# A gated state-space layer on one core: bounds widened two tiles ahead, and the carried state kept on 128 rows

## The chip, the cores and the metric

The kernel runs on one core of one Trainium2 chip. The metric is the device time of one execution in microseconds (us). PE is the matrix engine (PEld its weight loads), DVE the vector engine, ACT the scalar engine, POOL the general-purpose engine, and SP the engine whose queue issues the DMAs. Each engine runs its own instructions in order and waits on semaphores for the others.

## What is computed

Two sequences of 2048 tokens (512 features) go through a gated layer with 1024 inner features and a state of 16 x 1024 per sequence:

```python
xr, gate = jnp.split(x @ W_in.T, 2, axis=-1)
xr = xr + t_emb[:, None, :]
xc = silu(causal_depthwise_conv4(xr) + b_conv)
xn = layernorm(xc) * ln_g + ln_b
Bm, Cm, dt = jnp.split(xn @ W_xproj.T, 3, axis=-1)      # 16 each
Ad = 1.0 + 0.01 * tanh(dt @ W_dt.T + b_dt) * -tanh(A_log)
Bd = Bm * minimum(norm(xn), 1.0)
def step(h, inputs):                                     # h is 16 x 1024
    ad, bd, xt, ct = inputs
    h = clip(h * ad[:, :, None] + bd[:, :, None] * xt[:, None, :], -10.0, 10.0)
    return h, einsum('bd,bdh->bh', ct, h)
y = scan(step) + D * xn
out = x + (y * silu(gate)) @ W_out.T
```

## The kernel before

The tokens are cut into 32 chunks of 128 (the two sequences take turns). A chunk has 1024 x 16 scans, cut into 32 tiles: tile number u*4+q holds feature block u (128 features on the partitions) and states 4q to 4q+3, each over 128 tokens, so a tile is 128 x 512. One loop body per chunk `k` has 32 **steps** `s`, and every engine walks through them in its own order. A step has two **points**, 2s and 2s+1.

The way of one tile:

- PE `fill` (L538, four matmuls): the lower bounds of the scan into one of five PSUM banks, `ps_fill`. At step s it fills tile s+3 (`AHEAD`); it first waits for `scanned` of the tile five before (`RING`).
- ACT `copy_low` (L778): copies that bank to `low`. This is the first thing ACT does in a step, for tile s+3. After it come the side jobs of the step's two points.
- PE `widen` (L547, one matmul): adds the width of the bounds to the bank, so that it holds the upper bounds. It waits for `low_copied` of its tile. It is the first thing PE does in a step, ahead of `fill`. Before, step s widens tile s+1.
- DVE `scan` (L984): a max/min scan over `low` and the bank. DVE scans tile s+1 at step s.
- POOL `weigh` (L1082): times C, into one of `HOLD` = 4 buffers `prod`; a buffer is free when its tile is flipped.
- PE `flip` (L574, four transposing matmuls that sum into `ps_y`): tile s-4 at step s. Two tiles (0 and 16) are flipped one step later, together with the next.

Between these stand PE's other matmuls, by the table `JOBS` of (first point, number of parts, name, half, chunk offset, ...): PE does the part of an even point ahead of the step's flip, and that of an odd point behind it. They prepare the next two chunks: `xr` and `gate` (L450, L455, input projection), `conv` (L468, transposes of the taps), `xt`, `z`, `zT`, `nb` (L475), `carry` (L478), and close the last one: `hend` (L482, the state at a chunk's end), `yT`, `out` (L492). They share two banks, `ps_job`; a job waits till the job before it in its bank is taken. `TAKE` gives the point at which ACT or DVE takes a result, and `TAP_AT` the eight points at which ACT makes the four taps of a conv block (L737, into one of `TAPRING` = 3 buffers).

The state between chunks is `h1`, 16 rows x 1024. `hend` turns the chunk's last columns (`kend`) with 8 transposes, and DVE subtracts `lend` in two halves (L891). The job `h0` has a bank and no matmul: ACT writes `x0` times the first B into the bank (L704; `x0` is token 0 of the normalized input, sent by a DMA to 16 rows), DVE adds `h1` times the first decay (L918) and clips to `h1` (L931), again in two halves at points 16 to 22. The second half's L704 waits till the first half's L931 is done. ACT and POOL then split `h1` into two half-precision parts (L722, L1055).

Of the kernel before, what the change touches and what calls it, by code (L numbers as in the profile page):

```python
# [42 lines left out]
HOLD = 4  # L43
TAPRING = 3
# [25 lines left out]
xT_in xT_high xT_low tap_done conv_part x0_in0 x0_in1 spans_clear w_piece0 w_piece1 w_piece2 w_piece3 w_high w_low  # L70
# [10 lines left out]
y_gated h0_sum carry16  # L81
h0_ready h0_taken h1_in0 h1_in1 decay0 h1_high h1_low
# [3 lines left out]
def build(nc, A, out, scratch, r_dram, c_dram):  # L86
    F, H = mybir.dt.float32, mybir.dt.float16
    ALU, ACT = mybir.AluOpType, mybir.ActivationFunctionType
    with ExitStack() as S:
# [17 lines left out]
        small = sb("small_sb", [NS, 3 * NS + 2])  # L107
# [33 lines left out]
        first_decay = sb("first_decay", [NS, 1])  # L141
# [12 lines left out]
        h1 = sb("h1", [NS, DI])  # L154
        lend = sb("lend", [NS, 2, DI])
# [4 lines left out]
        h16 = sb("h16", [NS, 2, DI], H)  # L160
        x0 = h16[:].rearrange("n h d -> n (h d)").bitcast(F)
# [11 lines left out]
        kend = sb("kend", [P, 2, DB, NS])  # L173
# [24 lines left out]
        JOBS = [(3, 2, "z", 0, 1, 1, 1), (3, 4, "gate", 0, 0, 2, 0), (6, 1, "hend", 0, -1, 2, 1),  # L198
                (8, 4, "gate", 1, 0, 2, 0), (8, 1, "hend", 1, -1, 2, 1), (10, 1, "yT", 1, -1, 2, 1),
                (15, 1, "zT", 0, 1, 1, 1), (19, 4, "xr", 0, 2, 2, 0), (16, 1, "h0", 0, 1, 2, 1),  # L200
                (25, 4, "xr", 1, 2, 2, 0), (21, 1, "h0", 1, 1, 2, 1), (25, 1, "nb", 0, 1, 1, 1),
                (33, 11, "conv", 0, 2, 2, 0), (30, 1, "carry", 0, 1, 2, 1), (35, 1, "carry", 1, 1, 2, 1),
                (40, 13, "out", 0, -1, 1, 1), (46, 9, "conv", 1, 2, 2, 0), (54, 1, "yT", 0, 0, 2, 1),
                (57, 1, "xt", 0, 2, 2, 0), (60, 1, "xt", 1, 2, 2, 0)]
        LAST = {(name, i): first + parts - 1 for first, parts, name, i, *_ in JOBS}
        TAKE = {("z", 0): 5, ("gate", 0): 7, ("hend", 0): 6, ("hend", 1): 8, ("yT", 1): 10, ("gate", 1): 12,
                ("zT", 0): 15, ("h0", 0): 16, ("h0", 1): 20, ("xr", 0): 23, ("nb", 0): 25,
                ("xr", 1): 29, ("carry", 0): 30, ("carry", 1): 35, ("conv", 0): 44, ("out", 0): 53,
                ("conv", 1): 55, ("yT", 0): 54, ("xt", 0): 58, ("xt", 1): 62}
        TAP_AT = [26, 31, 33, 36, 39, 42, 45, 49]  # L210
# [52 lines left out]
        def first_chunk(j):  # L263
            return isinstance(j, int) and j < BATCH
# [10 lines left out]
        def _(sp):  # L275
            for dst, src in ((c128[:], A["c128"]), (cols[:], A["cols"]),
                             (wx, A["wxT"].rearrange("(c p) m -> p c m", p=P)), (small[:], A["small"]),
                             (h1[:], A["wx_dt"])):
                sp.dma_start(dst, src).then_inc(sem["const_in"], 16)
# [26 lines left out]
            def body(k, p):  # L306
# [21 lines left out]
                if exists(k, 1):  # L328
                    j, pn = k + 1, (p + 1) % 2
                    xstack, stack = sem[f"xstack_in{pn}"], sem[f"stack_in{pn}"]  # L330

                    since(sp, "filled", TILES * k)


                    sp.wait_ge(sem["xn_done"], j + 1)
                    sp.wait_ge(sem["xh_done"], j + 1)
                    if exists(k, 0):
                        sp.wait_ge(sem[f"h1_in{p}"], N_H1 * pair(k, p, 0))
                    sp.dma_start(x0, xn[0:1, pn].rearrange("o (n d) -> o n d", n=1).broadcast_to([1, NS, DI])).then_inc(sem[f"x0_in{pn}"], 16)
                    for jj in range(NSUB):  # L340
                        a = SUB * jj
                        sp.dma_start(xs[0:SUB, pn, jj], xh[a:a + SUB]).then_inc(xstack, 16)
                        sp.dma_start(xs[SUB:2 * SUB, pn, jj], xh[a:a + SUB]).then_inc(xstack, 16)
                    sp.wait_ge(sem["xl_done"], j + 1)
                    for jj in range(NSUB):
                        a = SUB * jj
                        sp.dma_start(xs[2 * SUB:3 * SUB, pn, jj], xl[a:a + SUB]).then_inc(xstack, 16)
                if exists(k, 1):
# [31 lines left out]
                    for jj in range(NSUB):  # L380
                        a = SUB * jj
                        for r, half in ((0, tth), (SUB, ttl), (2 * SUB, tth)):
# [3 lines left out]
                                         half[a + lead:a + SUB].rearrange("s n t -> s (n t)")).then_inc(stack, 16)  # L386
                    sp.wait_ge(sem["carry_taken"], 2 * j + 2)
# [16 lines left out]
            sp.wait_ge(sem["c_out"], 16 * STEPS)  # L404

        @block.tensor
        def _(pe):
# [20 lines left out]
            def job(k, p, m, part):  # L428

                _, parts, name, i, off, per, bank = JOBS[m]  # L430
                if not exists(k, off) or name == "h0":
                    return
# [64 lines left out]
            def inputs(j, q, name, i):  # L497
# [66 lines left out]
            def flip(k, p, s):  # L564
# [8 lines left out]
                for e in range(QN):  # L573
                    last = mm(ps_y[:, cut], prod[:, s % HOLD, e, :], ident, start=False,  # L574
# [37 lines left out]
        def _(act):  # L612
# [21 lines left out]
            def side(k, p, point):  # L634
# [47 lines left out]
                for _ in at("zT", 1, 1):  # L682
                    take("zT", 0, 1, 1)
                    since(act, "weighted", k + 1)
                    copy(zT[:], bank("zT")[0:NS, 0:2 * P].rearrange("n (e t) -> n e t", e=2)
# [24 lines left out]
                if point == 22 and exists(k, 1):  # L710
# [7 lines left out]
                if point == 41 and exists(k, 1):  # L718
                    act.wait_ge(sem["h0_taken"], 2 * (k + 2))
# [30 lines left out]
                for i in at("carry", 1):  # L750
# [4 lines left out]
                    since(act, "hend_taken", 2 * k)  # L755
                    copy(lend[:, 1 - p, half], bank("carry", i)[0:NS]).then_inc(sem["lend_set"], 1)
# [39 lines left out]
        def _(dve):  # L796
# [53 lines left out]
            def side(k, p, point):  # L850
# [30 lines left out]
                for i in range(2):  # L881
                    if point != TAKE["hend", i] or not exists(k, -1):
                        continue

                    half = slice(i * BANK, (i + 1) * BANK)
                    dve.wait_ge(sem["hend_ready"], 2 * (k - 1) + i + 1)
                    dve.wait_ge(sem["lend_set"], 2 * k)
# [3 lines left out]
                    stt(h1[:, half], lend[:, (k - 1) % 2, half], -1.0,  # L891
                        bank("hend", i)[0:NS], ALU.mult, ALU.add).then_inc(sem["hend_taken"], 1)
# [17 lines left out]
                for i in range(2):  # L910
                    if point != TAKE["h0", i] + 1 or not exists(k, 1) or first_chunk(j):
                        continue

                    half = slice(i * BANK, (i + 1) * BANK)
                    dve.wait_ge(sem["h0_ready"], 2 * j + i + 1)
                    dve.wait_ge(sem["hend_taken"], 2 * k)
                    dve.wait_ge(sem["decay0"], j + 1)
                    stt(bank("h0", i)[0:NS], h1[:, half], first_decay[:], bank("h0", i)[0:NS], ALU.mult, ALU.add  # L918
                        ).then_inc(sem["h0_sum"], 1)
                for i in range(2):  # L920
                    if point != TAKE["h0", i] + 2 or not exists(k, 1):
                        continue

                    half = slice(i * BANK, (i + 1) * BANK)
                    if first_chunk(j):
                        dve.wait_ge(sem["h0_ready"], 2 * j + i + 1)
                        since(dve, "h1_high", j)
                        since(dve, "h1_low", j)
                    else:
                        dve.wait_ge(sem["h0_sum"], 2 * (j - BATCH) + i + 1)  # L930
                    tsc(h1[:, half], bank("h0", i)[0:NS], CLIP, -CLIP, ALU.min, ALU.max  # L931
                        ).then_inc(sem["h0_taken"], 1)
# [3 lines left out]
                if point == 20 and exists(k, 1):  # L936
# [74 lines left out]
        def _(pool):  # L1011
# [4 lines left out]
            def body(k, p):  # L1016
                j, q = k + 1, (p + 1) % 2
                for s in range(TILES):
# [34 lines left out]
                    if s == 21 and exists(k, 1):  # L1053
# [19 lines left out]
            def weigh(k, p, i):  # L1073
# [8 lines left out]
                tt(prod[:, i % HOLD], ks[:, u % 2, part], crep[:, p, part], ALU.mult).then_inc(sem["weighed"], 1)  # L1082
# [46 lines left out]
```

## Time and profile before

| | |
|---|---|
| three runs, median | 2100.95 us (2098.36 to 2104.25) |
| the profiled execution, its own time | 2097.88 us |
| its span, first to last instruction | 2095.8 us |
| one chunk in the steady part | 61.96 us; eight of them, each with a stretch at half clock, 63.58 us |
| PE busy in such a chunk | 58.7 of 61.96 us |
| POOL, DVE, ACT busy in it | 56.2, 50.6, 44.4 us |
| DMA engines busy | 21.5% |

The trace has every instruction with its start, and for an engine's idle time the instruction that ended it. Successive matmuls overlap, so what one costs on PE is the distance from its start to the next start: 0.22 us for a 128x512 half-precision matmul, 0.44 us for the four of a flip. The chunk lengths are distances between equal instructions of successive chunks.

### The profile page before, as it was taken

What the parts mean: (1) busy time and instruction counts of PE and PEld (TensorE: products, weight loads), DVE (VectorE), ACT (ScalarE), POOL (GpSimd) and SP (SyncE); (2) the same over time, 40 slices, a digit from 0 to 9 for tenths busy, and PEclk for the clock granted to TensorE, in tenths of its full rate; (3) what the DMA queues carried; (4) which work ended last, traced back from release to release, by engine and by line L of the source; (5) the groups of instructions that cost most, each with busy time, mean ns of one, the idle gap of its engine ahead of it and who ended that gap; (6) DMA issues with size and microseconds to landing.
All of it is one profiled execution on the core that took longest, in us unless ns stands there. A gap on an engine that the chain in (4) does not pass through costs nothing.

```text
span 2095.8 us, 46902 instructions
## 1 busy us (share of the span) xinstructions
PE 1936.1 (92%) x16784; PEld 1466.0 (70%) x16784; DVE 1641.5 (78%) x2075; ACT 1439.5 (69%) x3494; POOL 1801.3 (86%) x1444
## 2 busy tenths in 40 slices
PE   5589999999999999999999999999999999999988
PEld 5467777777777777777677777777777777777765
DVE  3377887888877887878887888887888877888786
ACT  4677667777667777767777767677766777766753
POOL 1389988889988989898889998898998888998887
PEclk8699999999999999999999999999999999999999
DMA  5221222121222122222222222222122212222210
GB/s 174 56 61 43 62 46 61 55 66 47 58 46 61 55 66 51 55 45 63 58 61 54 54 54 55 57 59 61 48 62 46 61 55 61 48 61 47 56 50 16
DMA packets 83016, 120.16 MB, mean 57 GB/s; under 512 B 22352, under 2 KB 51408, under 8 KB 78112
## 3 DMA queue, kind: packets, MB, share of 16 engines
q1 hardware_dynamic: 82784, 117.17, 21.5%
q8 instruction: 133, 2.18, 0.4%
q14 instruction: 99, 0.81, 0.1%
HBM read 59.96 MB, written 9.18 MB: 33 GB/s over the span
## 4 chain that ended last, share of the span: by engine, by line
PE 64%; issue 11%; ACT 11%; DVE 10%; SPq 2%; POOL 1%; DMA 1%; DVEq 0%; ACTq 0%; POOLq 0%
PE ps_y L574 13%; PE ps_job L492 8%; PE ps_fill L547 7%; PE ps_job L455 7%; PE ps_fill L538 7%; PE ps_job L468 5%; PE ps_job L450 4%; DVE ks L984 3%; PE ps_y L554 3%; PE ps_y L560 3%; PE ps_job L462 3%; DVE h L931 2%; PE ps_job L478 2%; ACT xh L668 2%; ACT low L778 2%
## 5 line engine op out<-in xcount | busy, mean ns | idle before, releaser
L1082 POOL TENSOR_TENSOR prod<-ks,crep 128x512 f32<-128x512 f32 x1024 | 1289.2, 1279 | 187.8 <-PE ps_y L574 175.7
L984 DVE TENSOR_TENSOR_SCAN ks<-low,ps_fill 128x512 f32<-128x512 f32 x1024 | 1216.9, 1208 | 266.9 <-PE ps_fill L547 257.4
L778 ACT COPY low<-ps_fill 128x512 f32<-128x512 f32 x1024 | 590.1, 580 | 489.0 <-PE ps_fill L538 485.9
L574 PE MATMUL ps_y<-c_sb,prod 128*128 128x128 f32 x4096 | 613.5, 275 | 2.9 <-POOL prod L1082 1.4
L574 PEld LDWEIGHTS ps_y<-c_sb,prod 128*128 128x128 f32 x4096 | 464.3, 142 | 81.5 <-issue 45.0
L538 PEld LDWEIGHTS ps_fill<-ts,xs 128*128 128x128 f16 x4096 | 317.1, 99 | 172.3 <-issue 11.9
L538 PE MATMUL ps_fill<-ts,xs 128*128 128x128 f16 x4096 | 399.2, 220 | 11.7 <-DMA xs<-h 7.2
L547 PE MATMUL ps_fill<-spans,pick 128*128 128x512 f16 x1024 | 392.2, 383 | 6.8 <-ACT low L778 6.6
L450 PE MATMUL ps_job<-x,w_in 128*128 128x128 f16 x3072 | 226.8, 228 | 46.1 <-ACT xr L730 37.3
L737 ACT ACTIVATE tap<-xr,cols_sb 128x128 f32<-128x128 f32 x768 | 251.4, 391 | 16.3 <-PE ps_job L468 16.2
L450 PEld LDWEIGHTS ps_job<-x,w_in 128*128 128x128 f16 x3072 | 197.4, 103 | 59.6 <-issue 58.3
L455 PE MATMUL ps_job<-w_in,x 128*128 128x512 f16 x768 | 209.8, 383 | 10.6 <-ACT gate L662 10.6
L492 PE MATMUL ps_job<-w_out,yT 128*128 128x512 f16 x768 | 206.4, 379 | 1.5 <-DVE yT L898 1.5
L468 PE MATMUL ps_job<-c_sb,tap 128*128 128x128 f32 x1024 | 158.5, 280 | 9.1 <-ACT xc L744 5.2
L547 PEld LDWEIGHTS ps_fill<-spans,pick 128*128 128x128 f16 x1024 | 100.5, 98 | 65.7 <-ACT low L778 29.9
L468 PEld LDWEIGHTS ps_job<-c_sb,tap 128*128 128x128 f32 x1024 | 119.0, 145 | 23.6 <-ACT xc L744 5.8
L737 ACT ACTIVATE tap<-xr,conv_b,cols_sb 128x128 f32<-128x128 f32 x256 | 122.7, 479 | 0.0
L455 PEld LDWEIGHTS ps_job<-w_in,x 128*128 128x128 f16 x768 | 71.8, 104 | 48.4 <-issue 16.7
L492 PEld LDWEIGHTS ps_job<-w_out,yT 128*128 128x128 f16 x768 | 69.7, 98 | 35.1 <-DVE yT L898 1.7
L1030 POOL TENSOR_TENSOR xn<-xn,row_g 128x1024 f32<-128x1024 f32 x32 | 75.6, 2363 | 7.5 <-ACT xn L650 7.5
L1033 POOL TENSOR_TENSOR xn<-xn,row_b 128x1024 f32<-128x1024 f32 x32 | 75.4, 2355 | 0.2
L1055 POOL TENSOR_TENSOR h<-h 16x1024 f16<-16x1024 f32 x32 | 68.1, 2127 | 8.3 <-ACT h L722 8.3
(119 smaller groups left out, 2164.7 us busy)
## 6 DMA issues: line engine op xcount, KB each, us to landing
crep<-c_dram SPq DMA_DIRECT2D x32, 1024.0 KB, 4.8
xs<-xh SPq DMA_DIRECT2D x256, 64.0 KB, 2.7
xs<-xl SPq DMA_DIRECT2D x224, 64.0 KB, 2.0
xf<-in_xT SPq DMA_DIRECT2D x32, 256.0 KB, 2.8
res<-in_x SPq DMA_DIRECT2D x32, 256.0 KB, 2.7
out_dram<-res SPq DMA_DIRECT2D x32, 256.0 KB, 2.1
ts<-tth SPq DMA_DIRECT2D x128, 32.0 KB
ts<-tth SPq DMA_DIRECT2D x128, 31.0 KB
```

The source lines that it names most:

```text
L450: last = mm(ps[:, e * P:(e + 1) * P], w_in[:, a, c, d:d + P], x16[:, q, b, c, :], start=(c == n == 0), stop=(c == CB - 1 and n == 2))
L455: last = mm(ps, x16[:, q, a, c, :], w_in[:, b, c, DI + i * BANK:DI + (i + 1) * BANK], start=(c == n == 0), stop=(c == CB - 1 and n == 2))
L468: last = mm(ps[:, e * P:(e + 1) * P], tap[:, d % TAPRING, v], ident, start=(v == 0), stop=(v == TAPS - 1), is_transpose=True)
L492: last = mm(ps, yT[:, a, c, :], w_out[:, b, c, :], start=(c == n == 0), stop=(c == DB - 1 and n == 2))
L538: last = mm(o[:, :, SUB * jj:SUB * (jj + 1)], xs[:, p, jj, u * P:(u + 1) * P], ts[:, p, jj, q * QN * SUB:(q + 1) * QN * SUB].rearrange("s ...
L547: mm(ps_fill[:, (TILES * k + s) % RING], pick[:], spans[:, p, q * BANK:(q + 1) * BANK], start=False, stop=True, skip_group_check=True).the ...
L574: last = mm(ps_y[:, cut], prod[:, s % HOLD, e, :], ident, start=False, stop=(u % 4 == 3 and q == 3 and e == QN - 1), is_transpose=True)
L737: last = act_fn(tap[:, d % TAPRING, v], xr[:, p, d, v:v + P], ACT.Identity, scale=cols[:, d, 3 + v:4 + v], bias=conv_b[:, p, d:d + 1] if v ...
L778: copy(low[:, (TILES * k + s) % RING], ps_fill[:, (TILES * k + s) % RING]).then_inc(sem["low_copied"], 1)
L984: nc.vector.tensor_tensor_scan(ks[:, u % 2, QN * q:QN * (q + 1)].rearrange("d n t -> d (n t)"), low[:, g % RING], ps_fill[:, g % RING], 0. ...
L1030: tt(xn[:, p], xn[:, p], row_g[:], ALU.mult).then_inc(sem["xg"], 1)
L1082: tt(prod[:, i % HOLD], ks[:, u % 2, part], crep[:, p, part], ALU.mult).then_inc(sem["weighed"], 1)
```

## The change

- **Widening.** At step s PE widens tile s+2 in place of s+1. Filling is still three ahead, the banks are still five, and ACT's copies stand where they stood.
- **State on 128 rows.** `h1`, `h16`, `x0` become 128 x 128 (row = 8 times the state number + feature block). `hend` is one transpose and one DVE instruction; `lend` reaches 128 rows by a DMA. The job `h0` goes. In its place ACT puts the first B and the first decay side by side into `bd` (16 x 2), PE spreads them over 128 rows (job `bd`, one small matmul), and DVE multiplies, adds and clips on 128 x 128. `x0` goes out to DRAM and comes back over all rows.
- **Buffers.** `HOLD` 4 to 6, `TAPRING` 3 to 4.
- **Points.** The taps come 2 to 3 points earlier, the bounds' preparation (ACT) at 23 in place of 22 with `xr` half 0 taken at 22 in place of 23, `nb` at 26 in place of 25, `carry` one later, `out` from 41 in 12 parts in place of 40 in 13, the split of `h1` by ACT at 25 in place of 41, by POOL at step 16 in place of 21.

```diff
-HOLD = 4
-TAPRING = 3
+HOLD = 6
+TAPRING = 4
@@
-        JOBS = [... (6, 1, "hend", 0, -1, 2, 1), ... (8, 1, "hend", 1, -1, 2, 1), ...
-                (16, 1, "h0", 0, 1, 2, 1), ... (21, 1, "h0", 1, 1, 2, 1), (25, 1, "nb", 0, 1, 1, 1), ...
+        JOBS = [... (6, 1, "hend", 0, -1, 1, 1), ...
+                (19, 1, "bd", 0, 1, 1, 1), (26, 1, "nb", 0, 1, 1, 1), ...
@@
-        TAP_AT = [26, 31, 33, 36, 39, 42, 45, 49]
+        TAP_AT = [24, 28, 30, 34, 38, 40, 43, 46]
@@ SP
-                    sp.dma_start(x0, xn[0:1, pn].rearrange("o (n d) -> o n d", n=1).broadcast_to([1, NS, DI])).then_inc(sem[f"x0_in{pn}"], 16)
+                    sp.dma_start(x0_dram, xn[0:1, pn]).then_inc(sem["x0_out"], 16)
...
+                    sp.wait_ge(sem["x0_out"], 16 * (j + 1))
+                    since(sp, "bd_taken", j)
+                    sp.dma_start(x0[:], x0_dram.broadcast_to([NS, DI])).then_inc(sem["x0_in"], 16)
...
+                    sp.wait_ge(sem["lend_set"], 2 * j + 2)
...
+                    sp.dma_start(lend128[:, pn], lend[:]).then_inc(sem[f"lend_in{pn}"], 16)
@@ PE
-                    for e in range(4):
-                        last = tr(ps[0:NS, e * P:(e + 1) * P], kend[:, q, 4 * i + e, :], ident)
+                    last = tr(ps[:, 0:P], kend[:, q].rearrange("d n e -> d (n e)"), ident)
+                elif name == "bd":
+                    last = mm(ps[:, 0:2], spread, bd[:], start=True, stop=True)
@@ PE, body
                 for s in range(TILES):
-                    if s + 1 < TILES and exists(k, 0):
-                        widen(k, p, s + 1)
-                    elif s + 1 == TILES and exists(k, 1):
-                        widen(k + 1, 1 - p, 0)
+                    if s + 2 < TILES and exists(k, 0):
+                        widen(k, p, s + 2)
+                    elif s + 2 >= TILES and exists(k, 1):
+                        widen(k + 1, 1 - p, s + 2 - TILES)
@@ ACT
+                    copy(bd[:, 0:1], bank("zT")[0:NS, 0:1]).then_inc(sem["bd0_set"], 1)
...
-                for i in at("h0", 1):
...
-                    act_fn(bank("h0", i)[0:NS], x0[:, i * BANK:(i + 1) * BANK], ACT.Identity, scale=zT[:, 0, 0:1]
-                           ).then_inc(sem["h0_ready"], 1)
@@ DVE
-                    stt(bank("h0", i)[0:NS], h1[:, half], first_decay[:], bank("h0", i)[0:NS], ALU.mult, ALU.add
-                        ).then_inc(sem["h0_sum"], 1)
-                    tsc(h1[:, half], bank("h0", i)[0:NS], CLIP, -CLIP, ALU.min, ALU.max
-                        ).then_inc(sem["h0_taken"], 1)
+                    nc.vector.tensor_copy(bd128[:], bank("bd")[:, 0:2]).then_inc(sem["bd_copied"], 1)
+                    tsc(u, x0[:], bd128[:, 0:1], None, ALU.mult).then_inc(sem["u0_set"], 1)
+                        stt(u, h1[:], bd128[:, 1:2], u, ALU.mult, ALU.add).then_inc(sem["u1_set"], 1)
+                    tsc(h1[:], u, CLIP, -CLIP, ALU.min, ALU.max).then_inc(sem["bd_taken"], 1)
```

In a program's order of instructions a widening has no tile number, so its new place is seen best where the first chunk starts. PE before, the last steps ahead of chunk 0 (L459 is `xt`, L538 fill, L547 widen):

```order
L459 MATMUL ps_job<-c_sb,xc 128x128 x4
L538 MATMUL ps_fill<-ts,xs 128x4x32 x8
L459 MATMUL ps_job<-c_sb,xc 128x128 x4
L547 MATMUL ps_fill<-spans,pick 128x512
L538 MATMUL ps_fill<-ts,xs 128x4x32 x4
```

PE of the change at the same place (L469 `xt`, L552 fill, L561 widen):

```order
L469 MATMUL ps_job<-c_sb,xc 128x128 x4
L552 MATMUL ps_fill<-ts,xs 128x4x32 x4
L561 MATMUL ps_fill<-spans,pick 128x512
L552 MATMUL ps_fill<-ts,xs 128x4x32 x4
L469 MATMUL ps_job<-c_sb,xc 128x128 x4
L561 MATMUL ps_fill<-spans,pick 128x512
L552 MATMUL ps_fill<-ts,xs 128x4x32 x4
```

A bank is now widened with one fill between its own fill and its widening, before with two; from here on every step has one widening and one fill, as before.

ACT before, steps 7 to 11 of a chunk in the middle (L778 copy of `low`, L685 to L696 the taking of `zT`, L704 `h0`, L715/L717 bounds, L728/L730 `xr`):

```order
L778 COPY low<-ps_fill 128x512
L685 COPY zT<-ps_job 16x256
L687 ACTIVATE ad<-ps_job,small_sb 16x128
L690 ACTIVATE ad<-ad,unit,a 16x128
L696 ACTIVATE first_decay<-ad,p_end 16x1
L778 COPY low<-ps_fill 128x512
L704 ACTIVATE ps_job<-h,zT 16x512
L778 COPY low<-ps_fill 128x512
L709 COPY p_end<-pf 16x1
L773 COPY kend<-ks 128x16
L778 COPY low<-ps_fill 128x512
L704 ACTIVATE ps_job<-h,zT 16x512
```

ACT of the change there (L786 copy of `low`, L701 to L711 the taking of `zT`, L735/L737 `xr`, L722/L724 bounds):

```order
L701 COPY zT<-ps_job 16x256
L703 ACTIVATE ad<-ps_job,small_sb 16x128
L706 ACTIVATE ad<-ad,unit,a 16x128
L711 ACTIVATE bd<-ad,p_end 16x1
L786 COPY low<-ps_fill 128x512 x2
L716 COPY p_end<-pf 16x1
L781 COPY kend<-ks 128x16
L786 COPY low<-ps_fill 128x512 x2
L735 COPY xr<-xr 128x4x3
L737 ACTIVATE xr<-ps_job 128x4x128
L722 ACTIVATE ad<-pf 16x128 x2
```

The two L704 between the copies are gone, and `xr` stands ahead of the bounds.

## Rows read from the trace of the kernel before

**Rows 1.** The page's part 1: busy time, share of the span, instructions.

```profile
PE 1936.1 (92%) x16784; PEld 1466.0 (70%) x16784; DVE 1641.5 (78%) x2075; ACT 1439.5 (69%) x3494; POOL 1801.3 (86%) x1444
```

**Rows 2.** Stretches: start:end, length, busy us (instructions) per engine, granted clock, DMA, GB/s.

```profile
968.00:1029.96 61.96, 58.72 (x524) 44.50 (x523) 50.62 (x65) 44.37 (x110) 56.22 (x46) 1.00 0.22 57
...
1061.10:1064.50 3.40, 3.40 (x29) 3.26 (x28) 2.58 (x9) 2.65 (x10) 3.19 (x3) 0.50 0.00 0
999.20:1002.60 3.40, 3.40 (x53) 3.27 (x52) 3.37 (x10) 2.99 (x11) 3.40 (x3) 1.00 0.02 5
```

**Rows 3.** Waits: who waited for whom, us in total, times, longest.

```profile
ACT low L778 <- PE ps_fill L538: 485.9, 359, 5.1
DVE ks L984 <- PE ps_fill L547: 257.4, 334, 2.2
POOL prod L1082 <- PE ps_y L574: 175.7, 151, 3.7
...
PE ps_job L450 <- ACT xr L730: 37.3, 32, 1.2
...
PE ps_job L475 <- DVE h L931: 37.2, 30, 4.5
...
PE ps_job L455 <- ACT gate L662: 10.6, 31, 0.3
```

**Rows 4.** Timeline of PE, one chunk: start, duration, line, tiles [idle before].

```profile
971.79 0.39 PE L547 MATMUL ps_fill<-spans,pick 128*128 128x512 f16 x1 [0.17 <-ACT low L778]
...
985.74 0.38 PE L547 MATMUL ps_fill<-spans,pick 128*128 128x512 f16 x1
...
986.62 0.38 PE L547 MATMUL ps_fill<-spans,pick 128*128 128x512 f16 x1
...
988.93 0.38 PE L547 MATMUL ps_fill<-spans,pick 128*128 128x512 f16 x1
...
994.81 0.61 PE L574 MATMUL ps_y<-c_sb,prod 128*128 128x128 f32 x4
996.62 0.83 PE L450 MATMUL ps_job<-x,w_in 128*128 128x128 f16 x12 [1.21 <-ACT xr L730]
998.55 0.48 PE L475 MATMUL ps_job<-bc 16*128 16x144 f32 x2 [1.09 <-DVE h L931]
...
1010.23 0.38 PE L547 MATMUL ps_fill<-spans,pick 128*128 128x512 f16 x1
```

**Rows 5.** Timeline of ACT in the same chunk: the copies of `low`.

```profile
971.17 0.56 ACT L778 COPY low<-ps_fill 128x512 f32<-128x512 f32 x1
...
986.38 0.59 ACT L778 COPY low<-ps_fill 128x512 f32<-128x512 f32 x1 [2.12 <-PE ps_fill L538]
...
988.06 0.59 ACT L778 COPY low<-ps_fill 128x512 f32<-128x512 f32 x1
...
989.96 0.56 ACT L778 COPY low<-ps_fill 128x512 f32<-128x512 f32 x1
...
1006.27 0.56 ACT L778 COPY low<-ps_fill 128x512 f32<-128x512 f32 x1
...
1008.00 0.56 ACT L778 COPY low<-ps_fill 128x512 f32<-128x512 f32 x1
...
1009.55 0.57 ACT L778 COPY low<-ps_fill 128x512 f32<-128x512 f32 x1
...
1011.30 0.56 ACT L778 COPY low<-ps_fill 128x512 f32<-128x512 f32 x1
```

**Rows 6.** Groups of instructions in two chunks (940 to 1065 us): count | busy, mean ns.

```profile
L1055 POOL TENSOR_TENSOR h<-h 16x1024 f16<-16x1024 f32 x2 | 4.3, 2128 | 0.0
...
L931 DVE TENSOR_SCALAR h<-ps_job 16x512 f32<-16x512 f32 x4 | 2.6, 653 | 0.0
...
L482 PE MATMUL ps_job<-c_sb,kend 128*16 128x128 f32 x16 | 2.4, 273 | 0.0
...
L950 DVE TENSOR_TENSOR mT<-ps_job,c_sb 128x128 f32<-128x128 f32 x2 | 0.6, 281 | 0.0
```

More of the change, by code:

```diff
@@ L430, in job @@
                 _, parts, name, i, off, per, bank = JOBS[m]
-                if not exists(k, off) or name == "h0":
+                if not exists(k, off):
                     return
@@ L573, in flip @@
                 for e in range(QN):
[L574 removed]
+                    last = mm(ps_y[:, cut], prod[:, (TILES * k + s) % HOLD, e, :], ident, start=False,
                               stop=(u % 4 == 3 and q == 3 and e == QN - 1), is_transpose=True)
@@ L754, in side @@
                     copy(ch[:, half], bank("carry", i)).then_inc(sem["carry16"], 1)
-                    since(act, "hend_taken", 2 * k)
-                    copy(lend[:, 1 - p, half], bank("carry", i)[0:NS]).then_inc(sem["lend_set"], 1)
+                    if exists(k, 0):
+                        act.wait_ge(sem[f"lend_in{p}"], 16 * pair(k, p, 0))
+                    copy(lend[:, half], bank("carry", i)[0:NS]).then_inc(sem["lend_set"], 1)
                 if point == 27 and exists(k, 1):
@@ L880, in side @@
                         ).then_inc(sem["z_taken"], 1)
[L881 to L887, printed above, removed]
+                if point == TAKE["hend", 0] and exists(k, -1):
+                    dve.wait_ge(sem["hend_ready"], k)
+                    dve.wait_ge(sem[f"lend_in{1 - p}"], 16 * pair(k, p, -1))
                     if exists(k, 0):
@@ L890, in side @@
                         dve.wait_ge(sem["h1_low"], k + 1)
-                    stt(h1[:, half], lend[:, (k - 1) % 2, half], -1.0,
-                        bank("hend", i)[0:NS], ALU.mult, ALU.add).then_inc(sem["hend_taken"], 1)
+                    stt(h1[:], lend128[:, 1 - p], -1.0, bank("hend")[:, 0:P], ALU.mult, ALU.add
+                        ).then_inc(sem["hend_taken"], 1)
                 for i in range(2):
@@ L909, in side @@
                                                  ALU.mult, ALU.add).then_inc(sem["scan_p"], 1)
[L910 to L917, printed above, removed]
-                    stt(bank("h0", i)[0:NS], h1[:, half], first_decay[:], bank("h0", i)[0:NS], ALU.mult, ALU.add
-                        ).then_inc(sem["h0_sum"], 1)
[L920 to L924, printed above, removed]
+                if point == TAKE["bd", 0] and exists(k, 1):
+                    u = bank("bd")[:, P:2 * P]
+                    dve.wait_ge(sem["bd_ready"], j + 1)
+                    dve.wait_ge(sem["x0_in"], 16 * (j + 1))
+                    nc.vector.tensor_copy(bd128[:], bank("bd")[:, 0:2]).then_inc(sem["bd_copied"], 1)
+                    dve.wait_ge(sem["bd_copied"], j + 1)
+                    tsc(u, x0[:], bd128[:, 0:1], None, ALU.mult).then_inc(sem["u0_set"], 1)
+                    dve.wait_ge(sem["u0_set"], j + 1)
                     if first_chunk(j):
-                        dve.wait_ge(sem["h0_ready"], 2 * j + i + 1)
                         since(dve, "h1_high", j)
@@ L1081, in weigh @@
                 since(pool, "flipped", g - HOLD + 1)
-                tt(prod[:, i % HOLD], ks[:, u % 2, part], crep[:, p, part], ALU.mult).then_inc(sem["weighed"], 1)
+                tt(prod[:, g % HOLD], ks[:, u % 2, part], crep[:, p, part], ALU.mult).then_inc(sem["weighed"], 1)
             steps(body)
```

85 lines of the change are left out of this document (44 added, 41 removed), and 3 rows, old and new, of the table JOBS.

## The prediction

> **What bounds the kernel now.** I read the shares of busy time first, then one steady chunk, then the waits, then PE's and ACT's timelines of that chunk. PE is busy 58.72 of the 61.96 us of a chunk, POOL 56.22, DVE 50.62, ACT 44.37 [rows 1, 2]. The waits look large elsewhere: DVE waits 257 us for the widening, POOL 176 us for flips, ACT 486 us for fills [rows 3]. All three wait for PE, so these are the idle times of engines that PE leads. In that group PE's own waits are short: 37 us for `xr`, 37 us for the clip of `h0`, 11 us for `gate`. PE sets the pace, and a change counts by what it does to PE's queue.
>
> The timeline shows the two holes. PE starts `xr` half 1 at 996.62 where it was ready 1.37 us earlier (the flip before it began at 994.81 and costs 0.44), and `nb` at 998.55 where twelve 0.056 us matmuls after 996.62 would have let it in at 997.29: 1.26 us. Together 2.63 us a chunk [rows 4]. Both come from the `h0` chain: ACT's second L704 waits for DVE's clip, and that holds up ACT's `xr`; `nb` waits for the bank.
>
> The clock comes with it. In eight chunks a stretch just behind these two holes ran at a granted clock of 0.50 (1.2 GHz instead of 2.4), with 29 matmuls where 53 fit at 1.00 [rows 2]; such a chunk took 63.58 us, 1.62 more. All that the steady part has above 61.96 us a chunk is some 16 us.
>
> **Part 1, the state on 128 rows.** Off PE's path: POOL's subtraction goes from 2.13 us to about 0.3, six DVE instructions of about 0.65 us become five of 0.1 to 0.3 us, by a 128x128 row of 0.28 [rows 6]. ACT loses both L704. On PE's path: seven of eight `hend` transposes go, 0.109 us each (a flip's four cost 0.44), 0.77 us. Only half arrives: the first `hend` half stands ahead of `gate` half 1, which waits for ACT's `gate` anyway [rows 3]; its 0.33 us becomes a longer wait. Net -0.44. The new `bd` matmul is not in the trace; it costs more than nothing and less than the 0.48 us of `nb`'s two larger ones [rows 4]. It has 2 columns, so I take 0.1. The new ACT copy into `bd` costs 0.1. `x0` now leaves and comes back behind eight xs DMAs, about 5 us after its old place, and DVE wants it two steps later than before: by the timeline it is there some 4 us early. SP's added wait for `lend_set` holds up only three DMAs that wait for a later event, and the next chunk's first fill is ten steps off. If that cover failed, PE would stop at fill 0, at 2 to 3 us a chunk.
>
> The holes: `xr` is now taken before the bounds and no ACT instruction waits for DVE in front of it, so `xr` half 1 finds its bank free 0.3 us early; `nb` stands one step later and `bd` is taken some 4 us before it. Gain 2.63 us, the low bound 1.3 (one hole stays), the high 2.63.
>
> **Part 2, the widening.** Call P(s) PE's start of step s and A(s) the start of ACT's copy in it. When ACT is free the copy starts 0.64 us after P(s) (985.74 to 986.38), and its end lets PE widen about 0.64 us after A(s) (971.17 to 971.79) [rows 4, 5]. Before, widening tile s+2 stood in step s+1, so P(s+1) had to follow A(s-1) by 0.64. Now it must follow A(s) by 0.64: ACT loses a whole step of cover. Nothing is filled earlier to pay for it. A round trip is then 0.64 + 0.64 = 1.28 us, while a step with no job is 0.88 us (985.74 to 986.62) [rows 4]. Each such step stops PE 0.40 us even with ACT free. Where ACT is behind, it is worse, and I walked one chunk with P and A side by side: A(s+1) is the later of P(s+1) + 0.64 and A(s) plus ACT's work.
>
> - Steps 6 to 9. A(6) = P(6) + 0.64. ACT's steps 6 and 7 (gate, z, the input cast, the taking of `zT`) take 1.68 and 1.90 us by the distances 986.38, 988.06, 989.96, plus 0.1 for `bd`. P(9) = P(6) + 0.64 + 1.68 + 2.00 + 0.64 = P(6) + 4.96. Before it was 988.93 - 985.74 = 3.19 [rows 4, 5]. +1.77.
> - Steps 27 to 1. Light steps and the 1.15 us of `xn` on ACT: waits of 0.40, 0.66, 0.40 and 0.16, in all 1.62. Before, the same stretch had 0.98 us of waits, two on `xt` and one on the copy that ends at 971.73 [rows 4, 5]. +0.6.
> - Step 13: ACT has `xr`, bounds and a tap set behind one another, +0.43.
> - Steps 14 to 21. A tap set is 1.27 us of ACT (copy to copy 1006.27 to 1008.00 is 1.73, the copy itself 0.47), `carry` 0.97 (1008.00 to 1009.55). Before, tile 22's copy ends at 1011.30 + 0.56 = 1011.86, while the new place of its widening is 1010.23: 1.63 us late [rows 4, 5]. ACT's steps 14 to 20 take 2.48, 2.71, 0.48, 1.86, 1.44, 1.75 and 1.75 us; PE's 1.55, 1.53, 1.79, 1.32, 1.53, 1.32, 0.88. The walk gives waits of 0.68, 0.92, 0.29, 0.12 and 0.87; 0.16 of before go. +2.72.
> - Steps 21 to 27 have 1.5 to 4.8 us of PE work each and less of ACT: nothing.
>
> What it buys is that DVE scans about a step sooner, and with `HOLD` 6 POOL runs further ahead. No PE wait of any size is for a scan or a product [rows 3], so it buys 0. The fourth tap buffer frees no wait that the rows show.
>
> **The sum.** -0.44 (`hend`) + 0.1 (`bd`) - 2.63 (holes) + 0.43 (step 13) + 1.77 + 0.6 + 2.72 = +2.55; the walk, with its roundings, has +2.46, so 64.4 us a chunk. Thirty full chunks: +74. The clock's falls go with the holes, -16. The profiled execution of 2097.9 becomes 2156, and as that one was 3 us under the median of its runs, 2159.
>
> **Rivals.**
> A, the kernel gets faster: ACT catches up. The trace shows 15 us of ACT idle in a chunk on fills [rows 3], and it lost its `h0` pair, its wait and most of the cast of `h1`. If its lag at the copies never adds to the round trip, only the light steps cost: six waits of 0.4, 0.33 of `gate`, 0.1 of `bd`, 2.8 us a chunk. Against that stand the holes 2.63, `hend` 0.77, the old small waits 0.98 + 0.16 and the clock's 0.5, in all 5.0. So -2.2 us a chunk, times 31: 2033. It decides at 5.0 us of waits and new work a chunk; my walk has 7.4. Against it: ACT's work ahead of the late copies (the `zT` chain, the tap sets, `carry`) is all still there.
> B, about no change: half the lag is absorbed, 2100.
> C, the waits are right and the clock falls more. PE now has 2.0 us of waits in the 5 us of steps 6 to 9 and 2.9 us in steps 15 to 21. The rows show falls only behind a pair of holes of 2.63 us in 4. If one fall came in every chunk, 31 x 1.62 = 50 on top: 2209. Beside it: the Trainium skill, TensorE: Matmul & The Clock Gate, A second HAM failure mode, says that frequent short idles between matmul groups make the clock swing, which speaks against this change; by it the time is 2209, and the trace agrees so far that the clock fell without any single long gap.
> D, it doesn't do what it says: the earlier widening is held up by its own copy, so DVE scans hardly earlier. That is part of the forecast and has its time.
>
> **Chances.** Forecast with D 0.65, C 0.12, B 0.06, A 0.17. Range 2080 to 2215: it leaves out most of A and what is beyond C. A measurement can tell about 0.3% from no change: faster 0.18, same 0.05, slower 0.77.
>
> **What would show it.** A chunk of about 64.4 us; PE's waits for ACT's copy (L547 of before) up from 7 us to over 150, longest about 1.1, one behind the `zT` work and several among the taps; `xr` and `nb` holes near 0; ACT's wait for fills smaller per copy in light steps yet not gone; DVE waiting still for PE's widening; POOL's wait for flips smaller; the granted clock near 1.00. Wrong if PE's waits for the copy stay under 80 us, or if a new wait on `fill` 0 (DMA) appears.

## The result, and the profile after

The changed kernel takes 2186.38 us (median of 4, 2185.47 to 2186.76) against 2099.65 us: a ratio of 1.041, 95% interval 1.039 to 1.043. It is slower, as forecast, and 27 us slower than the 2159 forecast. A steady chunk takes 65.47 us in place of 61.96; the forecast had 64.4.

The page of the changed kernel, part 1, and one steady chunk as a stretch (they answer to [rows 1, 2]; the columns are the same):

```profile
PE 1941.9 (89%) x16624; PEld 1428.6 (65%) x16624; DVE 1599.8 (73%) x2045; ACT 1395.2 (64%) x3462; POOL 1749.2 (80%) x1444
```

```profile
1080.96:1146.43 65.47, 59.47 (x520) 43.89 (x518) 49.34 (x64) 43.12 (x108) 54.57 (x46) 1.00 0.19 54
```

Every engine has a smaller share of its time busy: in a chunk PE is busy 0.75 us more than before and the others less, and PE is idle 6.00 us in place of 3.24. The clock is 1.00, and no steady chunk has a fall: all 28 of them take 65.47 to 65.49 us. The waits of the changed kernel (they answer to [rows 3]; line 786 is the copy of `low`, 552 the fill, 561 the widening, 981 the scan, 588 the flip, 465 `gate`):

```profile
PE ps_fill L561 <- ACT low L786: 171.5, 334, 3.5
...
DVE ks L981 <- PE ps_fill L561: 104.8, 131, 2.3
...
POOL prod L1079 <- PE ps_y L588: 63.3, 98, 2.0
...
PE ps_job L465 <- ACT gate L676: 21.1, 31, 1.0
```

PE now waits for ACT's copy 334 times, 171.5 us in all, about ten times in a steady chunk. DVE's wait for the widening fell from 257 to 105 us, which is what the widening was moved for, and the time rose all the same. POOL's wait for flips fell from 176 to 63 us, but its wait for DVE's scans rose from 12 to 144 us, and the fall belongs to `HOLD`: in e2 below, which has the early widening and four buffers, POOL waits 274 us for flips, and in e1, with six buffers and the old widening, 4 us. The waits of `xr` and `nb` have left the list.

PE's timeline of the changed kernel, the last light steps of a chunk and the first of the next (start, duration, line, tiles [idle before]):

```profile
1072.34 0.38 PE L561 MATMUL ps_fill<-spans,pick 128*128 128x512 f16 x1
...
1073.62 0.39 PE L561 MATMUL ps_fill<-spans,pick 128*128 128x512 f16 x1 [0.23 <-ACT low L786]
...
1075.10 0.38 PE L561 MATMUL ps_fill<-spans,pick 128*128 128x512 f16 x1
...
1077.20 0.39 PE L561 MATMUL ps_fill<-spans,pick 128*128 128x512 f16 x1 [1.06 <-ACT low L786]
```

Step 29 runs from 1072.34 to 1073.62, 1.28 us: the round trip, to the digit (a step with no job was 0.88 in [rows 4]). ACT in the same place:

```profile
1072.98 0.59 ACT L786 COPY low<-ps_fill 128x512 f32<-128x512 f32 x1 [0.77 <-PE ps_fill L552]
...
1075.43 1.24 ACT L664 ACTIVATE xn<-xc,tiny 128x1024 f32<-128x1024 f32 x1 [0.57 <-DVE tiny L880]
1076.58 0.57 ACT L786 COPY low<-ps_fill 128x512 f32<-128x512 f32 x1
```

The copy starts 0.64 us after the step and ends just before the widening, with ACT idle ahead of it. Step 31 (1075.10 to 1077.20) has the longest wait of a steady chunk: ACT first waits 0.57 us for DVE's `tiny`, then makes `xn`, and only then the copy that PE stands waiting for.

**Where the time went, by step.** PE's start of a step, in us from the start of step 27 (the start of the step's widening in a steady chunk at full clock). The third column adds the prediction's terms to the column of before, each at the steps where the prediction puts it; they sum to 2.55, and the prediction's own 64.4 came from 2.46. The last column is the run e1_state_only, below.

| start of step | before | before and the prediction's terms | changed kernel | e1_state_only |
|---|---|---|---|---|
| 1 | 8.07 | 8.67 | 9.36 | 8.07 |
| 6 | 22.03 | 22.19 | 22.88 | 21.59 |
| 9 | 25.21 | 27.14 | 27.72 | 24.78 |
| 12 | 30.65 | 32.68 | 33.47 | 30.52 |
| 14 | 37.48 | 37.31 | 38.23 | 34.88 |
| 21 | 48.19 | 50.74 | 51.13 | 47.12 |
| 27 of the next chunk | 61.96 | 64.51 | 65.47 | 62.14 |

### The profile page after: what moved, and what is told of

Same layout as the page of the kernel before. It is cut to its first block, busy times and chain, and to the rows that moved or that the text cites. A ratio compares the mean times of both kernels' runs of the same rounds, so it can differ in the third digit from the quotient of the medians.

```text
span 2184.9 us, 46452 instructions
## 1 busy us (share of the span) xinstructions
PE 1941.9 (89%) x16624; PEld 1428.6 (65%) x16624; DVE 1599.8 (73%) x2045; ACT 1395.2 (64%) x3462; POOL 1749.2 (80%) x1444
## 4 chain that ended last, share of the span: by engine, by line
PE 56%; ACT 27%; issue 9%; DVE 5%; SPq 1%; POOL 0%; DMA 0%; ACTq 0%; DVEq 0%; POOLq 0%
PE ps_y L588 9%; ACT low L786 8%; PE ps_fill L561 8%; PE ps_job L503 8%; ACT tap L744 7%; PE ps_job L465 7%; PE ps_fill L552 7%; PE ps_job L460 6%; PE ps_job L478 3%; DVE ks L981 3%; PE ps_y L568 3%; PE ps_job L472 2%; ACT xh L682 2%; ACT gate L676 2%; PE ps_y L574 1%
## 5 line engine op out<-in xcount | busy, mean ns | idle before, releaser
L981 DVE TENSOR_TENSOR_SCAN ks<-low,ps_fill 128x512 f32<-128x512 f32 x1024 | 1202.3, 1205 | 108.2 <-PE ps_fill L561 104.8
L786 ACT COPY low<-ps_fill 128x512 f32<-128x512 f32 x1024 | 594.7, 581 | 674.1 <-PE ps_fill L552 671.1
L561 PE MATMUL ps_fill<-spans,pick 128*128 128x512 f16 x1024 | 393.4, 384 | 175.6 <-ACT low L786 171.5
L588 PEld LDWEIGHTS ps_y<-c_sb,prod 128*128 128x128 f32 x4096 | 457.8, 141 | 78.8 <-issue 50.6
L552 PEld LDWEIGHTS ps_fill<-ts,xs 128*128 128x128 f16 x4096 | 315.6, 98 | 159.6 <-issue 6.0
L552 PE MATMUL ps_fill<-ts,xs 128*128 128x128 f16 x4096 | 397.4, 220 | 4.3 <-DMA xs<-h 3.4
L561 PEld LDWEIGHTS ps_fill<-spans,pick 128*128 128x128 f16 x1024 | 99.2, 97 | 304.9 <-ACT low L786 212.5
L460 PE MATMUL ps_job<-x,w_in 128*128 128x128 f16 x3072 | 214.9, 221 | 10.3 <-POOL x L1049 7.8
L465 PE MATMUL ps_job<-w_in,x 128*128 128x512 f16 x768 | 204.0, 382 | 21.1 <-ACT gate L676 21.1
L460 PEld LDWEIGHTS ps_job<-x,w_in 128*128 128x128 f16 x3072 | 189.8, 99 | 12.7 <-issue 11.2
L961 DVE SCALAR_TENSOR_TENSOR xl<-xh,c_sb,ps_job 128x512 f16<-128x512 f16 x64 | 47.8, 747 | 136.5 <-ACT lend L764 136.5
L1024 POOL TENSOR_TENSOR tiny<-tiny,halfs 128x1 f32<-128x1 f32 x32 | 17.6, 549 | 115.4 <-DVE tiny L876 115.4
L902 DVE SCALAR_TENSOR_TENSOR yT<-ps_job,yT 128x512 f16<-128x512 f32 x64 | 44.3, 692 | 86.8 <-ACT yT L670 86.8
L1049 POOL TENSOR_TENSOR x<-xf,x 128x512 f16<-128x512 f32 x32 | 39.0, 1218 | 77.9 <-ACT x L695 77.9
```

What stands on the lines that cost most here:

```text
L460: last = mm(ps[:, e * P:(e + 1) * P], w_in[:, a, c, d:d + P], x16[:, q, b, c, :], start=(c == n == 0), stop=(c == CB - 1 and n == 2))
L465: last = mm(ps, x16[:, q, a, c, :], w_in[:, b, c, DI + i * BANK:DI + (i + 1) * BANK], start=(c == n == 0), stop=(c == CB - 1 and n == 2))
L552: last = mm(o[:, :, SUB * jj:SUB * (jj + 1)], xs[:, p, jj, u * P:(u + 1) * P], ts[:, p, jj, q * QN * SUB:(q + 1) * QN * SUB].rearrange("s ...
L561: mm(ps_fill[:, (TILES * k + s) % RING], pick[:], spans[:, p, q * BANK:(q + 1) * BANK], start=False, stop=True, skip_group_check=True).the ...
L588: last = mm(ps_y[:, cut], prod[:, (TILES * k + s) % HOLD, e, :], ident, start=False, stop=(u % 4 == 3 and q == 3 and e == QN - 1), is_tran ...
L786: copy(low[:, (TILES * k + s) % RING], ps_fill[:, (TILES * k + s) % RING]).then_inc(sem["low_copied"], 1)
```

## The experiments

All were timed against the kernel before on the same chip. Two questions: which part costs the time, and by what mechanism.

**The widening or the state?** e1 takes the widening back, e2 does it alone.

```diff
--- changed kernel, e1_state_only
-                    if s + 2 < TILES and exists(k, 0):
-                        widen(k, p, s + 2)
-                    elif s + 2 >= TILES and exists(k, 1):
-                        widen(k + 1, 1 - p, s + 2 - TILES)
+                    if s + 1 < TILES and exists(k, 0):
+                        widen(k, p, s + 1)
+                    elif s + 1 == TILES and exists(k, 1):
+                        widen(k + 1, 1 - p, 0)
--- kernel before, e2_widen_only: the same lines the other way round
```

> The change without its first part: PE widens tile s+1 at step s, as before; the state on 128 rows, the buffers and the points as in the change. Theory (the widening costs, the state part gains): the waits for ACT's copy fall from 172 us to under 15 us, both holes stay shut, the clock stays at 1.00, a chunk takes about 59 us and the run 1990 to 2010 us. Rival 1 (the state part itself costs, by its DMAs, its extra ACT copy and the moved points): 2100 us or more. Rival 2 (the early widening bought something through DVE and POOL, and only part of its cost is visible): new waits of PE for scans or products, 2040 us or more.

> The kernel before with only the widening moved: tile s+2 at step s. Theory: a chunk loses 4.5 to 6.5 us to waits for ACT's copy, the two holes of the h0 chain stay in part, the run takes 2240 to 2300 us. Rival 1 (the state part costs): at or below 2100 us. Rival 2 (the widening hurts only together with the earlier taps): 2100 to 2180 us.

e1: 2083.15 us, ratio 0.992 (0.991 to 0.994), 62.14 us a chunk. e2: 2217.59 us, ratio 1.056 (1.055 to 1.058), 66.32 us a chunk. The widening costs 119 us on the kernel before and 103 us on the changed one; the state part with its points and buffers gains 15 us alone and 31 us beside the widening. So the widening is the whole loss, and rival 1 of both texts is out. Both expectations missed on the number. e2 lies 22 us below my 2240 to 2300: it loses 4.36 us a chunk where I had 4.5 to 6.5, and part of the holes closed (steps 12 and 13 take 5.26 us in place of 6.83). e1 is 73 to 93 us above what I expected. Its holes are shut (steps 12 and 13 take 4.36 us), yet its waits for the copy are 50 us and not under 15, nearly all in front of steps 17 and 18, and between step 14 and step 22 it gives back 2.8 us, more than the 2.6 that it had won by step 14. Waits of e1, and ACT at step 13 (line 769 is ACT's work on the result of `nb`):

```profile
PE ps_fill L561 <- ACT low L786: 50.0, 89, 1.1
```

```profile
1118.96 0.57 ACT L786 COPY low<-ps_fill 128x512 f32<-128x512 f32 x1
1121.33 0.96 ACT L769 ACTIVATE bqm<-nbl,c_sb 128x32 f16<-128x32 f16 x4 [1.79 <-DVE nbl L945]
...
1122.30 0.57 ACT L786 COPY low<-ps_fill 128x512 f32<-128x512 f32 x1
```

ACT stands still 1.8 us for DVE's `nbl`, with five tap sets and two `carry` ahead. This wait is 56.3 us in e1 and 10.7 us in the changed kernel. That does not show that the early widening bought something. Counted from the start of step 27, DVE makes `nbl` at 35.93 us in e1 and at 37.38 in the changed kernel, so later and not sooner; the wait is short there because ACT arrives later still, held up by its own waits in the steps before. Rival 2 of e1 is right in number and in kind: PE has new waits for DVE (13.9 us for `gate`, 10.0 for `xl`), and ACT's wait for `nbl` reaches PE through the copies.

**The round trip, or ACT's backlog?** e3 exchanges fill and widening within PE's step; e4 fills a tile earlier.

```diff
--- changed kernel, e3_fill_first: order in each step
-                    widening of tile s + 2 (four lines)
-                    fill of tile s + 3 (four lines)
+                    fill of tile s + 3 (four lines)
+                    widening of tile s + 2 (four lines)
--- changed kernel, e4_fill_four_ahead
-AHEAD = 3
+AHEAD = 4
```

> The change with two lines of PE's step exchanged: fill of tile s+3 first, widening of tile s+2 behind it. The copy can then start 0.22 us sooner after the step's start and may end 0.22 us later, so the round trip is 0.43 us shorter (0.85 us, under the 0.88 us of a step with no job). Theory of the round trip: each of the dozen waits of a chunk shrinks by up to 0.43 us, 3 to 4 us a chunk, 2070 to 2100 us; steps 29 and 6 take 0.88 us in place of 1.28. Rival (ACT's backlog alone sets the pace, the round trip does not matter): within 20 us of 2186.

> The change with AHEAD 4 in place of 3: PE fills and ACT copies tile s+4 at step s, PE widens tile s+2; still five banks. ACT has its second step of cover back. Theory: the waits for the copy go, 1990 to 2030 us, and if the lead over the scan is worth anything it is below the run with one-ahead widening. Rival (five banks are too few for it): PE waits for scans at fill, tens of us in all, 2050 us or more.

e3: 2105.87 us, ratio 1.003 (1.002 to 1.004), 62.96 us a chunk. 80 us come back from an exchange that neither adds nor removes an instruction; it is 2.5 us a chunk where I expected 3 to 4, and the time is 6 us above my range. Steps 29 and 6 take 0.88 us in place of 1.28, as the round trip demands. The waits for the copy are still 117 us, now the backlog's:

```profile
PE ps_fill L561 <- ACT low L786: 116.9, 183, 4.0
```

e4: 2103.28 us, ratio 1.002 (1.001 to 1.003), 62.62 us a chunk, far from the 1990 to 2030 us of my theory. The waits for the copy are down to 8 us, and in their place PE waits at the fill for the scan of the tile that had the bank:

```profile
PE ps_fill L552 <- DVE ks L981: 70.6, 124, 9.1
```

The rival stated for e4 holds: five banks give ACT its step back only by taking it from DVE. No run had a sixth bank.

**What holds the state part back.** e5 to e8 start from e1. e7 puts each tap set back to its old point, 1 to 3 points later.

```diff
--- e1_state_only, e5_state_hold4
-HOLD = 6
+HOLD = 4
--- e1_state_only, e6_state_fill_first: fill of tile s + 3 ahead of the widening of tile s + 1
--- e1_state_only, e7_state_old_taps
-        TAP_AT = [24, 28, 30, 34, 38, 40, 43, 46]
+        TAP_AT = [26, 31, 33, 36, 39, 42, 45, 49]
--- e1_state_only, e8_state_half_taps
-                    for v in range(TAPS):
+                    for v in (0, TAPS - 1):
...
-                            last = mm(ps[:, e * P:(e + 1) * P], tap[:, d % TAPRING, v], ident,
+                            last = mm(ps[:, e * P:(e + 1) * P], tap[:, d % TAPRING, v // 2 * 3], ident,
```

> The state part with one-ahead widening (the run e1_state_only, 2083 us) and HOLD back at 4. PE flips tile s-4 at step s, so POOL has just enough buffers. Theory (POOL's wait for flips is idle time of an engine that PE leads): within 10 us of 2083, POOL's wait for flips up from about 0 to over 100 us. Rival (the spare buffers carry part of the gain): 2095 us or more.

> The run e1_state_only with fill ahead of widening in each step. Theory (in e1 PE waits where ACT's backlog of steps 12 to 21 reaches the copy): each of the four or five waits there shrinks by 0.2 us, 2050 to 2083 us. If the waits in e1 are the round trip, they can't be there with one-ahead widening (1.28 us against two steps), so nothing larger is expected. Rival (the order of the two costs elsewhere): above 2090 us.

> The run e1_state_only with TAP_AT of the kernel before, so only the points of ACT's tap sets move. By the copy-to-copy distances ACT then has about 1.3 us less work in steps 12 to 21. Theory (ACT's backlog there holds e1 at 62.1 us a chunk): 1 to 2 us a chunk less, 2025 to 2065 us. Rival (the backlog is in the bound and xr work of steps 11 to 13, or in DVE's lateness for nb): within 10 us of 2083.

> The run e1_state_only with two of the four tap activations of each conv block left out (PE transposes the same number of tiles, taking two of them twice, so the convolution is another one); ACT has 0.58 us less per block, 4.7 us a chunk. Theory (ACT's backlog): the 3.3 us of waits in steps 13 to 21 nearly vanish, a chunk takes about 59 us, 1985 to 2015 us. Rival (PE waits there for something else): above 2060 us.

e5: 2100.15 us, ratio 1.001 (1.000 to 1.002), 62.55 us a chunk; the rival holds: the spare buffers are worth 17 us, and I had called them worth nothing. POOL waits for flips 216 us, in e1 4 us, and ACT's wait for `nbl` is 66 us against 56. The traces show where the lateness passes from POOL to DVE. DVE's `pf` (the running product of the decays, L912) takes 1.14 us in e1 and 1.56 in e5, and in both it ends 0.27 us behind the `weigh` that POOL has under way or starts with it. First e1, then e5:

```profile
1048.27 1.27 POOL L1079 TENSOR_TENSOR prod<-ks,crep 128x512 f32<-128x512 f32 x1
1048.67 1.14 DVE L912 TENSOR_TENSOR_SCAN pf<-ad,spans 16x127 f32<-16x127 f32 x1
```

```profile
1116.76 1.28 POOL L1079 TENSOR_TENSOR prod<-ks,crep 128x512 f32<-128x512 f32 x1
1116.76 1.56 DVE L912 TENSOR_TENSOR_SCAN pf<-ad,spans 16x127 f32<-16x127 f32 x1
```

With four buffers POOL's `weigh` stands 0.41 us later there, and from `pf` to `nbl` DVE has no pause, so `nbl` and the whole chunk are 0.41 to 0.42 us later.

e6: 2066.86 us, ratio 0.985 (0.984 to 0.987), 61.5 us a chunk; inside the expected range.

e7: 2091.86 us, ratio 0.997 (0.996 to 0.998). My theory said 2025 to 2065; the rival (within 10 us of 2083) holds. A full-clock chunk is 62.14 us, just e1's, and four chunks with a clock fall, 7 us together, make up most of the rest. ACT still waits 49.5 us for `nbl`. PE's waits for the copy fell from 50.0 to 18.4 us, and its wait for DVE's `xl`, which stands behind the second `carry`, rose from 10.0 to 41.7 us:

```profile
PE ps_fill L561 <- DVE xl L961: 41.7, 30, 1.7
```

DVE starts that `xl` 46.26 us after step 27 in e1 and in e7 alike: between `nbl` and the second `carry` ACT makes three tap sets in both. So moving the sets took no work out of that stretch.

e8: 2029.20 us, ratio 0.967 (0.966 to 0.969), 60.38 us a chunk, 1.8 us less than e1. This lies between my range (1985 to 2015 us) and the rival's 2060: halving three sets takes 3 times 0.58 = 1.7 us, and the other five sets buy nothing.

**Filling the wait.** e9 puts a tap set where ACT stands still, e10 also moves three later ones, e11 puts the two-ahead widening back on e9.

```diff
--- e6_state_fill_first, e9_tap_in_wait
-        TAP_AT = [24, 28, 30, 34, 38, 40, 43, 46]
+        TAP_AT = [24, 27, 30, 34, 38, 40, 43, 46]
--- e6_state_fill_first, e10_taps_spread
+        TAP_AT = [24, 27, 30, 34, 38, 42, 45, 49]
--- e9_tap_in_wait, e11_two_ahead_best: widening of tile s + 2
```

> The run e6_state_fill_first (2067 us, 61.5 us a chunk) with ACT's second tap set at point 27 in place of 28, so that it stands in front of the work on nb's result in place of behind the next copy. In e1 ACT stands still 1.8 us there till DVE has made nbl. Theory (that wait starts ACT's backlog of steps 14 to 21): the wait shrinks by a tap set's 1.27 us, ACT's lag at step 16 falls from 4.4 to about 3.2 us, 0.8 to 1.3 us a chunk less, 2025 to 2045 us. Rival (the backlog is the sum of ACT's work and the place of a tap set doesn't matter): within 8 us of 2067.

> As e9_tap_in_wait, and the last three tap sets at points 42, 45, 49 (as in the kernel before) in place of 40, 43, 46, where ACT is idle a good part of steps 22 to 27. Theory: the waits of steps 18 and 20 shrink by some 0.4 us a chunk more, 2010 to 2035 us. Rival (they are waits for DVE's lateness with carry and gate, not for ACT's taps): the same as e9 within 8 us.

> The run e9_tap_in_wait (2030 us) with the widening two tiles ahead again; fill stands first, so the round trip is the short one. Theory: the waits for the copy behind ACT's longer steps come back (steps 0, 8, 16 to 18), while the wait for DVE's nbl that the moved tap set fills is small here anyway (13 us in e3 against 60 in e6), so this is 2085 to 2110 us, close to e3 with 2106, and the widening costs 60 to 75 us in this form. Rival (with the short round trip and the moved tap set, looking two ahead is harmless): under 2050 us.

e9: 2029.99 us, ratio 0.968 (0.966 to 0.969), 60.25 us a chunk. One point's move of one tap set brings 37 us. ACT in e9, at the place shown for e1:

```profile
1091.04 0.57 ACT L786 COPY low<-ps_fill 128x512 f32<-128x512 f32 x1
1091.52 0.98 ACT L744 ACTIVATE tap<-xr,cols_sb 128x128 f32<-128x128 f32 x3
...
1093.58 0.95 ACT L769 ACTIVATE bqm<-nbl,c_sb 128x32 f16<-128x32 f16 x4 [0.69 <-DVE nbl L945]
```

The tap set stands in the wait, 0.69 us of it is left, and PE's waits for the copy fall to 15 us:

```profile
PE ps_fill L561 <- ACT low L786: 14.9, 58, 0.3
```

e10: 2029.27 us, ratio 0.968 (0.966 to 0.969), the same as e9: its rival holds. The time is inside my range too, but the 0.4 us a chunk that I expected on top did not come; the last three tap sets do not make the waits that are left.

e11: 2091.81 us, ratio 0.997 (0.996 to 0.998), 62.49 us a chunk. With the short round trip and the moved tap set the two-ahead widening still costs 62 us. Waits of e11:

```profile
PE ps_fill L561 <- ACT low L786: 99.5, 154, 3.5
...
ACT bqm L769 <- DVE nbl L945: 2.8, 1, 2.8
```

ACT's wait for `nbl` is gone but for one, since ACT comes later than `nbl`, and PE has 99.5 us of waits for copies. e9 is the version to keep: 3.2% faster than the kernel before and 7% faster than the changed one.

**One chain through all of them.** The traces give, in a steady chunk at full clock, three times that add up to it: when DVE makes `nbl` (from the start of step 27), from there to DVE's second `xl`, and from there to the next step 27.

| run | `nbl` | to the second `xl` | to step 27 | chunk |
|---|---|---|---|---|
| e1 | 35.93 | 10.33 | 15.88 | 62.14 |
| e5, `HOLD` 4 | 36.35 | 10.33 | 15.88 | 62.55 |
| e6, fill first | 35.32 | 10.33 | 15.87 | 61.51 |
| e7, old taps | 35.93 | 10.33 | 15.88 | 62.14 |
| e8, half taps | 35.93 | 8.57 | 15.88 | 60.38 |
| e9 and e10, one set in the wait | 35.32 | 9.06 | 15.87 | 60.25 |
| e11, e9 with widening two ahead | 36.16 | 10.08 | 16.25 | 62.49 |
| changed kernel | 37.38 | 11.53 | 16.56 | 65.47 |

With one-ahead widening the last part is the same in every run, so a chunk is as long as the chain DVE `nbl`, ACT (its work on `nb`, the tap sets and both `carry`, without a pause), DVE `xl`. A whole tap set taken out of it is worth 1.27 us a chunk (e6 to e9), a set moved within it or behind it nothing (e7, e10). The two-ahead widening lengthens all three parts.

## Why the prediction was right, and where not

- **The bound.** That PE set the pace holds for the changed kernel: DVE's wait for the widening fell by 153 us and the time rose. It does not hold for the state part alone, where the chain above passes through DVE and ACT.
- **The rule for P and A.** A light step of 1.28 us, the copy 0.64 us after the step and the widening right behind it are in the timeline as written. e3 tests it apart from everything else: where the round trip is short, the light steps return to 0.88 us.
- **Steps 6 to 9.** Forecast P(6) + 4.96, measured 4.84.
- **Steps 27 to 1.** Forecast +0.6 us, measured +1.29, the largest part of the miss. The walk let `xn` start when ACT was free; it waited 0.57 us for DVE's `tiny`, and step 31 took 2.10 us in place of 1.54. The 0.98 us of old waits that the sum takes off were also too many: by the step starts only 0.73 go (0.40 in step 30, 0.33 in step 0).
- **The `bd` matmul.** Taken as 0.1 us between nothing and 0.48. Step 9 takes 1.96 us in the changed kernel and 1.56 in e2, which has no `bd`: 0.40 us. The term was taken from the wrong end. `nb` costs more at its new place too: step 13 takes 2.81 us, where its 2.23 of before and the 0.41 of `nb` make 2.64.
- **What the miss adds up to.** Against the terms' 2.55 us a chunk the trace has 3.51: 0.69 more in steps 27 to 1, 0.11 less in steps 6 to 9, 0.21 more in steps 9 to 12, 0.13 more in steps 12 to 14, 0.04 more behind them. Thirty chunks of that and the 0.09 lost in rounding to 2.46 are 31 us; the run missed by 27.
- **The holes.** They closed fully, as said, and the clock's falls went with them; PE's wait for `gate` grew from 11 to 21 us, as worked out for `hend`.
- **What is late next.** Here an argument failed though the sum held. The walk covered the changed kernel as a whole, and I entered all its added waits of steps 13 to 21 (0.43 and 2.72 us) under the widening, and the holes' 2.63 us under the state part. By these entries the state part alone gives 59.0 us a chunk; e1 takes 62.14. In the kernel before, DVE makes `nbl` 35.91 us after step 27 and the next step 27 comes 26.05 us later; in e1 it is 35.93 and 26.21. So closing PE's holes moved neither: a chain of almost the same length stood behind them. One reason is `pf`, which takes 0.41 us in the kernel before and 1.14 in e1, where it stands behind POOL. The state part is near nothing a chunk (62.14 against 61.96), and its 15 us are about what the clock falls cost before (eight times 1.62 us); the widening costs 3.3 us a chunk on top of it, or 4.4 on the kernel before. Because of that I expected 1990 to 2010 us of e1.
- **"It buys 0".** For the buffers this was wrong on e1: `HOLD` 6 is worth 17 us there. For the early widening no run shows a gain: with it `nbl` and the second `xl` come later, in the changed kernel and in e11. The rows of before did not show the part of POOL and DVE in the chain, as the long hole covered it.
- **Rival C** (one clock fall in every chunk) did not come: no fall in 28 steady chunks, though PE is idle 2.8 us more in each. The rule of the Trainium skill that I set beside it (TensorE: Matmul & The Clock Gate, A second HAM failure mode: short idles between groups make the clock swing) is not borne out by the changed kernel: eleven waits of up to 1.1 us a chunk left the granted clock at 1.00. The kernel before fell to 0.50 right behind its two holes, in nine of its steady chunks and not in the others, though all have the holes.
- **Rival A** needed ACT's lag not to add to the round trip. It does: steps 7 and 8 of the changed kernel take 1.69 and 1.87 us, more than the round trip's 1.28, and in e3, where the round trip is short, the lag alone still makes 117 us of waits.

## What to carry to other kernels

Looking further ahead in one stage of a pipeline, with the same buffers, takes the slack from the stage before it; measure the round trip (here fill, copy, widen: 1.28 us) against the shortest step first. An engine that waits long is no reason to serve it sooner when the engine that it waits for is the bound. When a stall is removed, walk the other engines through the time that it used to give them: a chain of nearly the same length may stand behind it, here through DVE and ACT. Find that chain first: the same tap set moved out of it was worth 37 us (e9), more than twice the edit that closed the stall, and moved within it nothing (e7).

## What the runs showed of the hardware

Exchanging two groups of instructions on PE, neither of which depends on the other (e3), was worth 80 us, 3.7%.

A pair of small matmuls with 2 columns of output (`bd`) took 0.40 us of PE's time; the pair with 144 columns (`nb`) took 0.41 us behind a hole and 0.58 us between other work. So most of the price is there with 2 columns already.

DVE's `pf` ended 0.27 to 0.28 us after the end of a POOL `weigh` in every steady chunk of the changed kernel and of the runs with the state part, and it lasted 1.05 to 1.57 us by how long that `weigh` still ran. In the kernel before and in e2 POOL was at the end of another instruction, and `pf` took 0.41 us.

In the steady chunks the granted clock fell from 1.00 to 0.50 in the kernel before (nine times, each in step 13, behind the waits of 1.21 and 1.10 us) and in four chunks of e7 (each in step 21, behind the wait of 1.37 us for `xl`); in the other chunks of both, with the same waits, it did not, nor in any of the other runs.
